# A pre-norm attention and expert block on one core: the second normalisation and all behind it two steps sooner, and three products moved inside the step

## The reference: what is computed

```
h = x + attention(LN(x)) @ Wo.T
y = h + experts(LN(h))

attention: 16 heads of 8 channels; a query sees itself and the 63 tokens before it in its sequence;
           softmax over scores * 8**-0.5
experts:   scores = sigmoid(z @ gate_kernel) + gate_bias, 16 experts in 4 groups; the 2 groups with
           the largest sum of their two best, then the 4 best experts of them, weights
           normalised and times 2.5
           sum over experts of weight * (silu(z @ w_gate) * (z @ w_up)) @ w_down   (64 hidden)
           + (silu(z @ sw_gate) * (z @ sw_up)) @ sw_down                           (128 hidden)
```

## Time and profile before

| | |
|---|---|
| median of three runs | 751.98 us (751.13 to 752.63) |
| the profiled execution | 752.66 us, of which the span is 750.8 us |
| busy in the span | PE 694.7, ACT 534.3, DVE 506.3, POOL 457.9 us |
| granted TensorE clock, mean | 0.977 |

### The profile page before, as it was taken

How to read it: one execution, slowest core, us unless ns; L and a number is a source line. 1 busy time by engine, 2 the same in 40 slices (tenths; PEclk the granted TensorE clock), 3 DMA queues, 4 the chain that set the end, 5 groups by cost and what they waited for, 6 DMA issues and landing times.

```text
span 750.8 us, 19358 instructions
## 1 busy us (share of the span) xinstructions
PE 694.7 (93%) x6256; PEld 570.6 (76%) x6256; DVE 506.3 (67%) x1584; ACT 534.3 (71%) x1603; POOL 457.9 (61%) x564
## 2 busy tenths in 40 slices
PE   3778789999999999999999999999999999896977
PEld 1667668787888888787888878788878888685855
DVE  2456575868677686858676776858686776876434
ACT  3676778787877778787878778787877778653322
POOL 5233156767767675767676676767677774344533
PEclk9998899999999999999999999999999999999889
DMA  5010022140403132130403131230404131222231
GB/s 165 1 30 29 1 79 80 41 132 4 141 28 114 56 102 68 58 112 11 131 28 118 51 114 56 73 96 26 130 14 130 39 114 44 71 87 68 76 100 43
DMA packets 50883, 53.63 MB, mean 71 GB/s; under 512 B 5792, under 2 KB 32032, under 8 KB 50720
## 3 DMA queue, kind: packets, MB, share of 16 engines
q1 hardware_dynamic: 50848, 53.18, 23.0%
HBM read 44.25 MB, written 4.72 MB: 65 GB/s over the span
## 4 chain that ended last, share of the span: by engine, by line
PE 73%; ACT 9%; DVE 9%; issue 4%; DMA 3%; POOL 1%; SPq 0%; POOLq 0%; DVEq 0%; ACTq 0%
PE PS L981 11%; PE PS L914 11%; PE PS L802 11%; PE PS L840 9%; PE PS L804 9%; PE PS L803 9%; ACT probs L567 5%; PE PS L828 3%; PE PS L944 3%; PE PS L927 2%; DVE neg_max L724 2%; PE PS L978 2%; DVE tu L716 2%; DMA spread<-weights_by_expert 2%; ACT cT L519 1%
## 5 line engine op out<-in xcount | busy, mean ns | idle before, releaser
L567 ACT ACTIVATE probs<-PS,neg_max 128x96 f32<-128x96 f32 (+1 forms) x1024 | 246.4, 349 | 91.0 <-DVE neg_max L724 91.0
L448 POOL TENSOR_TENSOR gate<-gate,spread 128x512 f32<-128x512 f32 x128 | 163.5, 1277 | 178.8 <-ACT gate L519 86.3
L716 DVE SCALAR_TENSOR_TENSOR tu<-th,PS 128x512 f32<-128x512 f32 x128 | 87.5, 684 | 104.3 <-ACT th L535 70.1
L981 PE MATMUL PS<-wd,hh 128*128 128x128 f32 x1024 | 138.2, 278 | 14.4 <-DVE OUT L730 11.8
L981 PEld LDWEIGHTS PS<-wd,hh 128*128 128x128 f32 x1024 | 128.4, 194 | 21.0 <-DVE OUT L730 12.8
L724 DVE TENSOR_REDUCE neg_max<-PS 128x4 f32<-128x384 f32 (+1 forms) x256 | 122.5, 517 | 21.8 <-PE PS L840 17.0
L453 POOL TENSOR_TENSOR hh<-gate,tu 128x512 f32<-128x512 f32 x100 | 127.8, 1278 | 7.8
L802 PE MATMUL PS<-x_hi,w_hi 128*128 128x512 f32 x288 | 125.5, 436 | 0.2 <-DVE tu L716 0.2
L535 ACT ACTIVATE th<-PS 128x512 f32<-128x512 f32 x128 | 79.7, 623 | 53.6 <-PE PS L804 52.0
L804 PE MATMUL PS<-x_lo,w_hi 128*128 128x512 f32 x288 | 115.1, 400 | 0.0
L702 DVE STREAM_TRANSPOSE probsT<-probs 128x768 f32<-128x768 f32 (+1 forms) x128 | 114.5, 894 | 0.0
(11 more groups left out here) (102 smaller groups left out, 954.9 us busy)
## 6 DMA issues: line engine op xcount, KB each, us to landing
spread<-weights_by_expert SPq DMA_DIRECT2D x256, 128.0 KB, 3.0
X<-x SPq DMA_DIRECT2D x32, 256.0 KB, 3.4
OUT<-H SPq DMA_DIRECT2D x16, 256.0 KB, 2.9
out<-OUT SPq DMA_DIRECT2D x16, 256.0 KB, 2.9
ffn_stage<-w_gu SPq DMA_DIRECT2D x1, 1152.0 KB, 5.3
wd<-w_down SPq DMA_DIRECT2D x1, 512.0 KB, 6.4
weights_by_expert<-cT SPq DMA_DIRECT2D x16, 32.0 KB, 1.6
probsT<-w_att SPq DMA_DIRECT2D x1, 192.0 KB, 3.1
```

Source lines behind the costliest of these rows:

```text
L448: tt(gate2[:, :], gate[:, k % 2, :], spread[:, k % SP_BUFS, :], ALU.mult).then_inc(s_g2, 1)
L567: ins = nc.scalar.activation(probs[:, u % 2, tt, 2 * rows + e, j0:KW], PS[:, rows, n * KW + j0:n * KW + KW], ACT.Exp, bias=neg_max[:, rows ...
L716: v_.scalar_tensor_tensor(tu[:, k % 2, :], th[:, :], 1.0, PS[:, 5, :], ALU.add, ALU.mult).then_inc(s_tu, 1)
L981: ins = mm(PS[:, 7, r], hh[:, k % 2, r], wd[:, k, :], start=(k == 0 and n == 0), stop=(k == NP - 1), skip_group_check=True)
```

## The change

The numbers of the stages XT2, LG, RT, CT, FF, DN and YE become smaller by two, that of LN2 by one, and that of SH grows by two. KP takes step 5, QP step 6, VP step 7, and VB goes from steps 7 and 8 to 10 and 11. On PE the logits LG stand behind the scores, followed by QP and CT; KP stands behind PV; VP and XT2 stand near the end of a step. On DVE, LN2 stands behind OW, VP behind YE, XT2 behind `turn_probs`. On ACT, `x2_hi` and the key copies stand behind the exponentials, and the logits' tanh stands between their halves. PE runs 24 matmuls of 4 x 4 before its first wait. The places in `USES` are ordered anew. The core of the diff:

```diff
 LN1 = 3
 XT = 4
-QP, KP, VP, VB = 5, 6, 6, 7
+KP, QP, VP, VB = 5, 6, 7, 10
 SC = 8
 TR = 9
 PV = (12, 13, 16, 17)
 OE = 13
 OT, ON, OW = 14, 15, 16
-LN2 = 17
-XT2 = 19
-LG = 24
-RT = 24
-CT = 27
-SH = 25
-FF = 28
+LN2 = 16
+XT2 = 17
+LG = 22
+RT = 22
+CT = 25
+SH = 27
+FF = 26
 SP_BUFS = 4
-DN = 29
-YE = 37
+DN = 27
+YE = 35
 RING = (3, 6)
-EARLY, POST, LATE, WEIGHTS = range(4)
+EARLY, MID, POST, LATE, LAST = range(5)
 USES = sorted([(stage % STEPS, place, stage) for place, stages in (
-    (EARLY, (VP, LG)), (LATE, (XT, QP, KP, XT2, XT2 + 4, SH)),
-    (POST, (OT, OT + 4, ON, ON + 4, OW, OW + 4, SH)), (WEIGHTS, (CT,)))
+    (EARLY, (LG,)), (MID, (QP,)), (LATE, (XT, VP, XT2, XT2 + 4, SH)),
+    (POST, (KP, CT, OT, OT + 4, ON, ON + 4, OW, OW + 4)), (LAST, (SH,)))
     for stage in stages])
 assert len({use[:2] for use in USES}) == len(USES)
...
+WARM = 24
...
+                        if g:
+                            side, bank = filled(act, sl, s, EARLY)
+                            nc.scalar.activation(th_r[:, :], bank[:, 0:NT * E], ACT.Tanh,
+                                                 scale=0.5).then_inc(s_taken[side], 1)
                         g, _ = at(sl, s, SH)
...
                         if rows == 0:
                             between_halves()
+                    g, b = at(sl, s, XT2, 4, GB)
+                    if g:
+                        side, bank = filled(act, sl, s, LATE)
+                        copy(x2_hi[:, g.par, T * b:T * b + T], bank[:, 0:T]).then_inc(s_high[side], 1)
+                    g, _ = at(sl, s, KP)
+                    if g:
+                        if g.fixed and g.n == 0:
+                            act.wait_ge(s_pool, 7)
+                        side, bank = filled(act, sl, s, POST)
+                        for e in range(2):
+                            ins = copy(k_by_row[:, g.par, e, :], bank, scale=keyrow[:, e:e + 1])
+                        ins.then_inc(s_taken[side], 1)
...
-                            taken(act, slot_before(sl) if s == 0 else sl, VP % STEPS, EARLY)
+                            taken(act, slot_before(sl), VP % STEPS, LATE)
                         for v in (2 * half, 2 * half + 1):
                             ins = copy(v_bd[:, g.par, :, :, 0, D * v:D * v + D].rearrange("p n g d -> p (n g) d"),
...
+                            dve.wait_ge(s_vb, g.n)
+                        v_.transpose(v_keys[:, :, :, :].rearrange("p n g d -> p (n g d)"), bank
+                                     ).then_inc(s_taken[side], 1)
                     for place in range(2, 8):
                         routing(sl, s, place)
-                    g, b = at(sl, s, LN2, 4, GB)
-                    if g:
-                        taken(dve, sl, (OW + 4 * b) % STEPS, POST)
...
+                    if g:
+                        taken(dve, sl, (OW + 4 * b) % STEPS, POST)
+                        stats(sl, H2[:, g.par, 2 * b:2 * b + 2, :], 2, st2, mv2).then_inc(s_mv2, 1)
+
+                    g, _ = at(sl, s, LN1)
...
+                    turn_probs()
                     g, b = at(sl, s, XT2, 4, GB)
                     if g:
                         side, bank = high_out(sl, s, LATE)
...
+            pe.wait_ge(s_pool, 1)
+            for _ in range(WARM):
+                mm(PS[0:NT, 7, 0:NT], half_neg[:, :], half_neg[:, :], start=True, stop=True)
             pe.wait_ge(s_w, 16 * LOADS)
...
+
+                    g, _ = at(sl, s, LG)
+                    if g:
+                        side, bank = free(EARLY)
+                        taken(pe, sl, (XT2 + 4) % STEPS, LATE)
+                        if g.fixed and g.n == 0:
+                            pe.wait_ge(s_cst, 4)
+                        for n in range(NT):
+                            r = slice(P * n, P * n + P)
+                            ins = exact3(bank[:, E * n:E * n + E], x2_hi[:, g.par, r], x2_lo[:, g.par, r],
+                                         *w2(GK, E))
+                        ins.then_inc(s_filled[side], 1)
+
+                    g, _ = at(sl, s, QP)
+                    if g:
+                        side, bank = free(MID)
+                        exact3(bank, *w2(WQ), xT_hi[:, :], xT_lo[:, :]).then_inc(s_filled[side], 1)
+                    g, _ = at(sl, s, CT)
+                    if g:
+                        side, bank = free(POST)
+                        pe.wait_ge(s_cb, g.n + 1)
+                        for n in range(NT):
+                            ins = nc.tensor.transpose(bank[0:E, P * n:P * n + P], comb[:, n, :], ident)
+                        ins.then_inc(s_filled[side], 1)
                     for turn_, stage in enumerate(PV):
...
+                    g, _ = at(sl, s, KP)
+                    if g:
+                        side, bank = free(POST)
+                        taken(pe, sl, XT % STEPS, LATE)
+                        exact3(bank, *w2(WK), xT_hi[:, :], xT_lo[:, :]).then_inc(s_filled[side], 1)
...
                         x2 = x2_hi[:, g.par, :], x2_lo[:, g.par, :]
-                        for place, n in ((POST, WG), (LATE, WU)):
+                        for place, n in ((LATE, WG), (LAST, WU)):
                             side, bank = free(place)
...
-                    g, _ = at(sl, s, QP)
+                    g, _ = at(sl, s, VP)
                     if g:
                         side, bank = free(LATE)
-                        taken(pe, sl, XT % STEPS, LATE)
-                        exact3(bank, *w2(WQ), xT_hi[:, :], xT_lo[:, :]).then_inc(s_filled[side], 1)
-                    g, _ = at(sl, s, KP)
-                    if g:
...
+
                     g, k = at(sl, s, DN, 1, NP)
                     if g:
                         if k == 0 and not (g.fixed and g.n == 0):
...
-                            ins = nc.tensor.transpose(bank[0:E, P * n:P * n + P], comb[:, n, :], ident)
+                    g, b = at(sl, s, XT2, 4, GB)
+                    if g:
+                        side, bank = free(LATE)
+                        pe.wait_ge(s_xn2, g.n * GB + b + 1)
+                        for n in range(2):
+                            ins = nc.tensor.transpose(bank[:, P * n:P * n + P], xn2[:, n, :], ident)
                         ins.then_inc(s_filled[side], 1)
```

More of the change, by code:

```diff
@@ L582, in slot @@
                     if g:
-                        if g.fixed and g.n == 0:
-                            act.wait_ge(s_pool, 7)
-                        side, bank = filled(act, sl, s, LATE)
+                        side, bank = filled(act, sl, s, MID)
                         for v in range(4):
                             ins = copy(q_by_head[:, g.par, :, v, :], blocks(bank), scale=queryrow[:, v:v + 1])
-                        ins.then_inc(s_taken[side], 1)
-                    g, _ = at(sl, s, KP)
-                    if g:
-                        side, bank = filled(act, sl, s, LATE)
-                        for e in range(2):
-                            ins = copy(k_by_row[:, g.par, e, :], bank, scale=keyrow[:, e:e + 1])
                         ins.then_inc(s_taken[side], 1)
@@ L703, in turn_probs @@
                                          probs[:, u % 2, :, :, c0 * Q:KW]).then_inc(s_pt, 1)
-                    g, _ = at(sl, s, VP)
-                    if g:
-                        side, bank = filled(dve, sl, s, EARLY)
-                        if not (g.fixed and g.n == 0):
-                            dve.wait_ge(s_vb, g.n)
-                        v_.transpose(v_keys[:, :, :, :].rearrange("p n g d -> p (n g d)"), bank
-                                     ).then_inc(s_taken[side], 1)
                     g, k = at(sl, s, FF, 1, NP)
@@ L731, in slot @@
                                          ALU.add).then_inc(s_y, 1)
+                    g, _ = at(sl, s, VP)
+                    if g:
+                        side, bank = filled(dve, sl, s, LATE)
+                        if not (g.fixed and g.n == 0):
+                            dve.wait_ge(s_vb, g.n)
+                        v_.transpose(v_keys[:, :, :, :].rearrange("p n g d -> p (n g d)"), bank
+                                     ).then_inc(s_taken[side], 1)
                     for place in range(2, 8):
                         routing(sl, s, place)
[L734 to L737 removed]
                     g, b = at(sl, s, OT, 4, GB)
@@ L847, in slot @@
                 for s in range(STEPS):
-                    if sl.fixed and sl.n == 0 and s == QP:
+                    if sl.fixed and sl.n == 0 and s == KP:
                         pe.wait_ge(s_cst, 2)
```

69 lines of the change are left out of this document (16 added, 53 removed).

## The result

The kernel after takes 776.56 us (median of four runs, 775.24 to 777.2) against 752.31 us of the kernel before beside it: ratio 1.0319, 95% interval 1.0295 to 1.0343. It is slower, as forecast, but by 24 us and not by 4, and it lies outside the range that I gave.

A forecast was written before the change was run, and what follows sets the result against it. TensorE, busy 93% of the span, was taken to bound the kernel. Loop +20.3, start -2.3 and drain -13.8 gave +4.2 us against the profiled 752.66, 0.7 above the 751.98 median: forecast 756, range 738 to 768.

The forecast's parts named there:

- Part 1: Loop, step 3: late value copies delay the sum OUT, so PE waits before the first down product, 1.2 us a slot.
- Part 2: Loop, step 6: the first o transpose waits for the gate logits' bank, held until their late tanh, 0.7 us a slot.
- Part 3: Loop, step 0: VectorE's added work in step 7 makes PE wait for probsT, 0.3 us a slot (0 to 0.6).
- The old 0.64: Loop: PE's existing waits for step 3's exponentials (0.45) and x2_lo (0.19) go, 0.64 us a slot.
- Loop, in sum: Slots 4 to 16: 2.2 us of new waits less 0.64, +1.56 a slot, times 13 slots, +20.3 us.
- Part 4: Start: keys first -1.8, values' copies +0.5, earlier feed-forward filling waits -1.0 at step 28; -2.3 us in all.
- Part 5: Drain: two steps fewer, shorter waits for OUT and no clock fall, -13.8 us (between -9 and -18).
- Part 6: Beginning: the 24 matmuls of 4x4 take 2.7 us while PE has nothing to do; cost 0, no gain.
- Rival 1: Loop: ScalarE not late in step 3, the sum comes in time, ends are won; 736.7 or 741 us; chance 0.27.
- Rival 2: Loop: waits feed each other through the spread loads, 2.5 us a slot or more; 769 up to 780; chance 0.12.
- Rival 3: Drain: not won, spread loads stay the bound at both group ends; 764 us; chance 0.06.
- Rival 4: Start: the early matmuls keep the clock up, 5 us less; 751, no change; chance 0.05.

The follow-up runs named there:

- e5: The kernel after with the last sum (YE, OUT) first in VectorE's step, ahead of tu and neg_max: 766.75 us.
- e1: The kernel after with the values by head (VB) copied in steps 0 and 1 instead of 2 and 3: 772.01 us.
- b1: The kernel before with only the copies of the values by head moved, to steps 2 and 3 from 7 and 0: 765.65 us, ratio 1.0178.
- c6: The kernel after with OUT's sum and turn_probs early, logits' tanh ahead of the exponentials, value copies split between steps 0 and 3: 745.85 us, ratio 0.9917.
- e2: The kernel after with the gate logits' tanh ahead of the exponentials on ScalarE instead of between their halves: 768.03 us.
- e4: The kernel after with one more matmul of 448 columns, its result unused, ahead of the gate logits: 768.62 us.
- e3: The kernel after with turn_probs on VectorE right behind the sum OUT, ahead of values, routing and second normalisation: 765.09 us.
- c1: The kernel after with both VectorE edits, e5 and e3, together: 765.0 us.
- w0: The kernel after without the 24 small matmuls at its beginning: 774.59 us, ratio 1.0307.
- c4: The kernel after with OUT's sum and turn_probs early (c1) and all four value copies in step 0: 753.51 us, ratio 1.0014.

## Why the prediction was wrong

The sign and the waits of the loop were right; the size was not. The profiled executions differ by 22.7 us of span: +3.1 in the start, +32.2 in the 13 slots, -12.7 in the drain. Forecast were -2.3, +20.3, -13.8. Of the 18.5 us that are missing, some 8.4 are falls of the clock in the loop, 5.4 are in the start, 3.8 in the slots at the upper clock and 1.1 in the drain.

**Part 1 (OUT, +1.2).** 0.53 for `OUT` and 0.31 for `oT` in the same place make 0.84. The place and the lateness of tanh (2.40 forecast, 2.42 measured) were right. What I did not see is that `OUT` only covers other late work: with the sum early, PE waited 0.4 for `v_bd` (e5), and with the copies early 0.7 for `probs` (e1). The root is the copies, as b1 shows.

**Part 2 (th_r, +0.7).** Measured 0.55, 13 times. The size was right; what hangs on it was missed: the clock fell behind it in six slots.

**Part 3 (probsT, +0.3).** 0.44, within its bounds.

**The old 0.64.** Gone, as forecast.

**The term that no part had: PE's busy time.** +0.66 a slot at the upper clock. The last matmul ahead of a wait is not overlapped by the next: of 512 columns it counts 0.40 instead of 0.23 us, 0.17 more ahead of each of the waits for `oT`, `OUT` and `th_r`, and the scores 0.07 more ahead of the one for `probsT`. That is up to 0.58. It goes with the wait: in e5, without the one for `OUT`, a slot is busy 41.76 instead of 41.94. With nearly all waits gone (c6) 0.27 stay, which I take for the new order itself. The sum is 1.83 + 0.66 - 0.64 = 1.85 a slot against 1.56 forecast, and 24.1 us over 13 slots against 20.3: within the bounds given, and nearer than its terms, since the new waits were forecast at 2.2 and came to 1.83 while this term stood at nothing.

**Loop, in sum: the step that failed.** It took every slot at the upper clock, as the slots before had been. Six slots fell to the lower level, 1.3 to 1.5 us each, 8.4 us in all, and e2 and e4 removed them both without making a slot of the first kind shorter. I had priced the clock in the start and in the drain, where it was seen low, and not where a new wait was being put.

(The 8.4 are from one profiled execution of the kernel after; e2 and e4 bear them out, 8.5 and 7.9 us less in the medians.)

**Part 4 (start, -2.3), the second step that failed.** The -1.8 of the keys came as forecast (16.66). The term that failed is the -1.0 at step 28. Its own numbers do not give it: 4.8 us of work against some 3 of waiting and 1.4 is +0.4, so the start should have stood at -0.9. And of the some 3 us of waiting that feed-forward was to fill, PE filled 1.1 between steps 24 and 28, with 3.9 us more to do: +2.8. The rest was lost before: I booked nothing for the later slots of the start, while LN2, now in the step of OW and so ahead of that step's `turn_probs`, brought waits for `probsT` of 1.19, 0.69 and 0.57, where the kernel before had two of 0.41 and 0.53. With `turn_probs` early again the start is 1.6 shorter (e3), with OUT's sum early as well 2.5 (c1), and in c6 it is 103.0, the 102.8 of before. The two steps of feed-forward that I meant to hide in waits are so not won in any version. Why PE still waits 2.66 us in these four steps no run tested. More stays open: the granted clock between 20 and 46 us was 0.70 in after and 1.00 in before, but in e4 it was 1.00 too and the start 1.4 longer, so the clock there is not what decides.

**Part 5 (drain, -13.8).** -12.7. The two long waits are 2.59 and 3.27 instead of 5.37 and 5.15; I had 1.4 and 3.5. Why the first is 1.2 above my 1.4 was not tested and stays open; the work that I laid beside the chain adds up to 8.95 us and not to 8.7, which makes the miss 1.4. In c6 it is 2.31, but there PE also waits 0.67 for `comb` ahead of the transposes of the weights, so that says little. The clock did not fall behind the first (the down product took 1.16 us), as I took it; behind the second it did (1.49, then 0.77 for 512 columns).

**Part 6 (the early matmuls, 0).** Right for the whole, as far as w0 tells; they took 1.35 us and not the 2.7 I took. The Trainium skill ("TensorE: Matmul & The Clock Gate", section "Why this matters for your kernels") says to warm TensorE up first. In this kernel the rule gives nothing in the form it was applied: between the tiny matmuls and the first real one lay a wait of 6.4 us, and the first product ran at the 1.2 GHz level with them and without.

**The rivals.** Rival 1 named the right test, tanh of step 3 under 1.3 us after PE's gate product; it was at 2.4. Rival 2 was the nearest by its time (769 to 780), but its mechanism did not happen: in the loop of the kernel after PE waits for no spread load. It was nearer than the forecast had it, though. GpSimd waits 4.62 us for one in step 2 (409.44), and the first `hh` is done at 412.09, 1.0 us before PE would take it; in c6, with the other waits gone, this chain is what PE waits for in nine slots. Rival 3: no. Rival 4: no; it was the same resource, the clock, with the other sign and in another place.

## What to carry to other kernels

When a change adds a wait to TensorE, price three things: the wait, the end of the matmul ahead of it that nothing overlaps any more (0.17 us here for 512 columns), and a fall of the clock behind it; here a quarter of the gross loss of the loop, 8.4 of 24.1 + 8.4 us by the table and the slots, was of the last kind. When several stages are moved, find the engine on which they queue (ScalarE here) and put its copies where it idles: one slot of its timeline tells where. Two copies in step 0 and two in step 3 were worth 5 us over four in step 0. Removing one late producer hands its wait to the next; only all of them together pay, so judge such edits by the slot's length and not by the wait that went. And look at the slots after a change that should do nothing, too: w0 had the same time as the kernel after, and a different loop.

## What the runs showed of the hardware

An added matmul of 448 columns made the kernel 8 us faster, and in its trace the granted clock stayed at its upper level in all 13 slots, of which six had had a fall; where nothing fell in the loop (c4) the same matmul won nothing. How long PE waits does not decide alone whether the clock falls: behind 0.55 us in step 6 it fell in every second slot or so, behind 0.55 us in the same place of c4 it did not in the loop. In the drain it did not behind 2.59 us (after) nor behind 2.89 (w0), but it did behind 3.27 (after), 2.38 (c6) and 1.82 (c4). How many slots fall also changes with edits elsewhere (six, three, four, seven, one), and I can't say from these runs what chooses them. A fall lasted some 3.5 us and cost 1.3 to 1.6 us. And PE can stand still in a loop without a wait that the profile shows: 1.27 to 1.67 us at every second slot of w0, which differs from the kernel after only by 24 matmuls ahead of the loop.
